# A two-layer gated cross-attention and mixture-of-experts kernel: loads in halves, grouped norms, tables asked early, and the first expert slot's columns by a permutation product

## Chip, cores and metric

One NeuronCore of a Trainium2 chip runs the whole program in one launch. The time is device microseconds (us) of an execution, the median of three runs.
## What is computed

The input x is 8 blocks of 128 tokens with 256 features; ctx_2048 has the same shape. All is float32.

```python
x = x + tanh(g_xattn[0]) * L0_xattn(layernorm(x), ctx)   # 16 heads of 16, softmax over 128 keys
x = x + tanh(g_ffn[0])   * L0_ffn(layernorm(x))          # 8 experts of 512, the best one per token
x = x + tanh(g_xattn[1]) * L1_xattn(layernorm(x), ctx)   # as L0, rms-normed queries and keys
x = x + tanh(g_ffn[1])   * L1_ffn(layernorm(x))          # causal attention 16x128, then top-6 of 16 experts
```

## The kernel before

**Stage 1, first cross-attention (0 to 89 us of the profile).** `xattn_pe`, `xattn_act`, `xattn_dve` and `xattn_pool` run with L = 0 over `steps()`, n from -3 to 8. The loop is pipelined over the blocks b: step n makes the scores of block n+1, turns the probabilities of block n (`pt`, L487), makes keys, queries and values of block n+2 (L445, L451) and turns the normalised rows of block n+3 (`normed`, L433). `first_turns` lists by hand which PSUM bank of 4 to 7 each product takes and who reads it. `keys` (ACT, L656) writes each head pair's keys masked, `queries` (L668) adds the bias; scores (L478) fill banks 0 to 3, and `softmax` (DVE, L834 and L835) reads them in two halves, subtracts the row maxima and so frees the banks for the next block's scores. `xattn_pool` makes the rows of the layer norm (`normed`, L816) from `rstd`, which `power` (L770) takes as x**-0.5 on POOL for a group of blocks at a time: for ln1 blocks 0 to 3, then 4 to 7, from `bn_stats` and `moments` that DVE makes ahead of the loop for all eight blocks. `powered` is the wait for such a group; the table POWERS gives the order.

SP issues all loads on one queue: x in two halves, the gates (16 bytes for each partition), ctx of block 0, all four weight matrices of layer 0 at once (`WX[0]`, 1 MB, semaphore wx_in[0]), `cols` (48 bytes for each partition), `vecs`, ctx of blocks 1 to 3, the router's weights, WX[1], and then the experts' weights WE. PE runs 24 products with zeros (`fill(24, 0)`, L334), then waits for WX[0] before anything else. ACT's first instruction is the tanh of the gates (L1971).

**Stage 2, first experts (89 to 216 us).** `ffn_act` and `ffn_dve` find each token's expert: exponentials (L1440), one-hot rows `hot`, the place of each token among those of its expert by products with the triangle `earlier` and with `ones` (PE, L1351 and L1353, bank 3), then `pos`, the row of each token in the list sorted by expert (L1517), and `ex`, the expert of each slot of 128 rows (L1524); there are 15 slots. `ffn_pool` waits for `pos` and scatters the 8 blocks of FX into `xs_d` in DRAM by 8 indirect DMAs (L1571); when all have landed, SP loads the rows of slots 0 and 1 (L1591), PE turns them into columns (`columns`, L1372) and the slots begin. In slot j, PE does gate product (L1378), the turn of slot j-1's hidden rows (`turn_hidden`, L1385), the columns of slot j+1 (L1372), the up product (L1378) and slot j-1's down product (L1393); gate and up take banks `par` and 2 + `par`.

While the scatter runs, PE makes keys and values of the second cross-attention for MOST = 6 blocks (`keys_values`, L1357, banks 4 to 7) from rT, for which SP loads all of ctx again once the router is done; DVE adds biases and squares (L1530, L1531, L757) and, when POOL has the power (L1574), scales the keys (`normalise_keys`, L1470). Fills of 8, 7, 10 and 2 stand around these. The last two blocks' keys and values come behind the slots.

POOL then gathers the 8 blocks from `ys_d` by indirect DMAs (L1581), with the keys' power behind block 2 and the power of ln3 for blocks 0 and 1 behind block 4. DVE's `add_experts` (L1476, L1477) adds each block to X as it lands; after blocks 6 and 7 it writes the normed rows of blocks 0 and 1 (L816), then `moments` of blocks 2 to 7, whose power POOL takes before its `normed(2)`.

**Stage 3, second cross-attention (216 to 301 us).** As stage 1 with L = 1; `fill(10, 7)` stands before it. ACT loads the activation table of the exponential on reaching the first `exps` (L676).

**Stages 4 and 5.** Causal attention (`attn_*`) and the 25 tiles of the last experts (`moe_*`), with three products for each float32r pair (L338 to L340). `moe_act` squares the columns (L1156), copies them (L1160), and loads the table of the silu on reaching the first one (L1170), for which PE's next product waits.

```python
pe.wait_ge(wx_in[0], 16)                     # stage 1, ahead of all products
sp.wait_ge(s.scattered, 16 * B)              # stage 2, SP
load(0, 0)
load(1, 1)
if b == FIRST + 2:                           # stage 2, POOL, in the loop of gathers
    power(pool, "ln3")
```

Of the kernel before, what the change touches and what calls it, by code (L numbers as in the profile page):

```python
# [23 lines left out]
P = 128  # L24
# [11 lines left out]
CTX = 4  # L36
# [3 lines left out]
J1 = SJ + E1 * I1 // P  # L40
VEC = ["bv0", "bo0", "bk1", "bv1", "bo1", "nk1"]
# [26 lines left out]
def build(nc, ctx_d, x_d, wx_d, vec_d, col_d, gate_d, rw0_d, rw1_d, moe0_d, moe1_d, attn_d, attnv_d, out_d):  # L68
    stack = ExitStack()
    with stack:  # L70
# [10 lines left out]
        WX = [sb(f"WX{i}", [P, C, 4 * D]) for i in range(2)]  # L81
# [18 lines left out]
        mhalf = sb("mhalf", [P, B])  # L100
        in_ms = sb("in_ms", [P, B])
# [46 lines left out]
        gs = [sb(f"gs{i}", [P, I0], where=e) for i in range(2)]  # L148
# [88 lines left out]
        x_in = [sem("x_in0"), sem("x_in1")]  # L237
        gate_in, vec_in, late_in, out_done = sem("gate_in"), sem("vec_in"), sem("late_in"), sem("out_done")
        wx_in = [sem("wx_in0"), sem("wx_in1")]
# [57 lines left out]
        class Es:  # L297
# [9 lines left out]
            h_ready, ht_done, ht_ready, d_done, y_ready = (sem("e_" + k) for k in ("h_ready", "ht_done", "ht_ready", "d_done", "y_ready"))  # L307
# [53 lines left out]
        def first_turns(n):  # L361

            early = [(name, 2, reader) for name, reader in (("K", "A"), ("V", "D")) if n == -1]
            late = [] if n == 0 else [("K", n + 2, "A")], [] if n == 0 else [("V", n + 2, "D")]
# [5 lines left out]
            return [*(routed(0, 1) if last else []), ("cxT", n - 1, "A"), *((f"P{i}", n, "A") for i in range(4)),  # L370
# [45 lines left out]
        def xattn_pe(pe, L):  # L416
            s, m_, W = xs[L], xbs[L], WX[L]
# [22 lines left out]
            def columns(name, b, w0, src):  # L440

                out = bank(name, b)
                for o in range(C):
                    for c in range(C):
                        m = nc.tensor.matmul(out[:, o * P:(o + 1) * P], W[:, c, w0 + o * P:w0 + (o + 1) * P], src[:, c, :], start=(c == 0), stop=(c == C - 1))  # L445
                m.then_inc(s.turn_done, 1)

            def rows(name, b, w0, src):
                out = bank(name, b)
                for c in range(C):  # L450
                    m = nc.tensor.matmul(out[:, 0:D], src[:, c, :], W[:, c, w0:w0 + D], start=(c == 0), stop=(c == C - 1))  # L451
                m.then_inc(s.turn_done, 1)

            def keys(b):
                pe.wait_ge(s.ctx_in[b % CTX], 16 * (b // CTX + 1))
                columns("K", b, 0, m_.cT[b % CTX])

            def queries(b):
                read("xT", b)
                columns("Q", b, 2 * D, m_.xT)  # L460
# [53 lines left out]
            def output(b):  # L514
                read("cxT", b)
                rows("O", b, 3 * D, m_.cxT)
# [19 lines left out]
            if L == 0:  # L536
                pe.wait_ge(Es.zeroed, 1)
                fill(24, 0)
                pe.wait_ge(psum_zeroed, 1)
                pe.wait_ge(wx_in[0], 16)  # L540
                for n in steps():
                    last, end = n == B - 1, n == B
                    if has(n + 1):
                        scores(n + 1)
                    if last:
# [18 lines left out]
                    if has(n + 2) and n != 0:  # L564
                        rows("V", n + 2, D, m_.cT[(n + 2) % CTX])
# [20 lines left out]
                    if n == -1:  # L586
                        keys(2)
                        rows("V", 2, D, m_.cT[2])
# [3 lines left out]
            fill(10, 7)  # L592
# [46 lines left out]
        def xattn_act(act, L):  # L639
# [42 lines left out]
            if L:  # L682

                for b in range(2):
                    act.wait_ge(Es.kt_free, b + 1)
# [3 lines left out]
                key_columns(act, MOST, B)  # L689
            def value_rows_back(n):  # L690
# [71 lines left out]
        POWERS = [("ln1", 0, EARLY), ("ln1", EARLY, B), ("ln2", 0, EARLY), ("ln2", EARLY, MOST), ("ln2", MOST, MOST + 1), ("ln2", MOST + 1, B), ("ln3", 0, FIRST), ("ln3", FIRST, B),  # L762
                  ("ln4", 0, B)]
        INPUTS = [(0, 2), (2, 4), (4, MOST), (MOST, MOST + 1), (MOST + 1, B)]

# [52 lines left out]
        def xattn_dve(dve, L, ch):  # L818
# [43 lines left out]
            if L == 0:  # L862
                for n in steps():
                    if has(n + 1):
                        softmax(n + 1, 0)
                    if has(n - 1) and n != B - 2:
# [3 lines left out]
                    if has(n + 2) and n != 0:  # L870
# [18 lines left out]
            for n in steps():  # L889
# [4 lines left out]
                if has(n + 1):  # L894
                    softmax(n + 1, 1)
                if B - 4 <= n < B:
# [17 lines left out]

        def xattn_pool(pool, L):
# [1183 lines left out]
```

## Time and profile before

| what | value |
|---|---|
| median of three runs | 778.97 us (778.62 to 780.02) |
| the profiled execution's own time | 778.13 us |
| its span (first to last instruction) | 776.4 us |
| mean granted TensorE clock | 0.991 of 2.4 GHz |
| PE busy | 742.0 us, 96% of the span |
| DVE, ACT, POOL busy | 54%, 44%, 32% |
| DMA | 58.04 MB, mean 75 GB/s |

Times in the profile run from the span's start. A line such as "20.38 1.15 PE PS L478 x16" is start, duration, engine, written tile, line and number of records. A float32 product leaves two records, so L478's 16 records are 8 products. The busy time of PE contains fills, products with zeros that no result needs.

### The profile page before, as it was taken

To read this page: it belongs to the slowest core of one execution; us is meant where nothing else is said; L and a number is where in the kernel's file an instruction comes from. 1 tells how busy PE (TensorE), PEld (TensorE's weight loads), DVE (VectorE), ACT (ScalarE), POOL (GpSimd) and SP (SyncE) were. 2 spreads that over 40 slices of the span, in tenths; PEclk is the share of its full clock that TensorE was granted. 3 is DMA by queue.
4 is the path that set the end of the run, shared out by engine and by line. 5 is a ranking of instruction groups with operands and counts; after the bars stand their busy time and mean duration, and the time that the engine had idled before them with its cause. 6 is when DMAs were issued, how large, how long until landed. Compare 5 with 4: busy or idle time off the path is not lost.

```text
span 776.4 us, 13496 instructions
## 1 busy us (share of the span) xinstructions
PE 742.0 (96%) x4636; PEld 605.4 (78%) x4637; DVE 421.1 (54%) x806; ACT 342.9 (44%) x813; POOL 248.7 (32%) x298
## 2 busy tenths in 40 slices
PE   8999989999869989999999999999989999999998
PEld 6787746666557767889988998898868888888886
DVE  6878451121467774544454445445564565656565
ACT  3888212222258773544454445444453332233223
POOL 5203240000444673732222321322223443444430
PEclk9999999999989999999999999999999999999999
DMA  8970221111300010101101100010014334333331
GB/s 315 420 278 2 55 81 35 47 41 41 109 15 2 1 35 1 35 22 55 35 20 34 54 20 34 20 62 21 0 41 126 97 119 115 115 114 102 115 101 55
DMA packets 25606, 58.04 MB, mean 75 GB/s; under 512 B 3536, under 2 KB 14416, under 8 KB 24288
## 3 DMA queue, kind: packets, MB, share of 16 engines
q1 hardware_dynamic: 24800, 55.42, 21.9%
q0 software_dynamic: 768, 2.10, 0.8%
q8 instruction: 25, 0.41, 0.2%
q14 instruction: 13, 0.11, 0.0%
HBM read 51.41 MB, written 6.09 MB: 74 GB/s over the span
## 4 chain that ended last, share of the span: by engine, by line
PE 80%; DVE 7%; ACT 6%; POOL 3%; DMA 2%; issue 2%; SPq 0%; DVEq 0%; POOLq 0%; ACTq 0%
PE PS L338 15%; PE PS L340 15%; PE PS L339 15%; PE PS L1636 7%; PE PS L1378 7%; PE PS L1393 3%; PE PS L445 3%; PE PS L478 2%; PE PS L487 2%; PE PS L451 2%; PE PS L1642 2%; PE PS L500 1%; POOL Z L816 1%; DVE x_mx L834 1%; PE PS L433 1%
## 5 line engine op out<-in xcount | busy, mean ns | idle before, releaser
L338 PE MATMUL PS<-tTh,wh 128*128 128x512 f32 x200 | 78.4, 392 | 1.4 <-ACT act_s L1170 0.9
L1181 ACT ACTIVATE hhh<-hh 128x512 fp32r<-128x512 f32 x50 | 31.6, 632 | 105.1 <-DVE hh L1207 94.7
L340 PE MATMUL PS<-tTh,wl 128*128 128x512 f32 x200 | 77.9, 390 | 0.0
L339 PE MATMUL PS<-tTl,wh 128*128 128x512 f32 x200 | 77.9, 389 | 0.0
L637 DVE TENSOR_TENSOR hhl<-hh,hhh 128x512 fp32r<-128x512 f32 x50 | 52.4, 1048 | 34.9 <-ACT hhh L1181 34.9
L1747 ACT ACTIVATE sm<-sm,nmx 128x128 f32<-128x128 f32 x128 | 49.6, 389 | 37.7 <-DVE nmx L1810 37.7
L1273 POOL CAST wh<-wraw 128x512 fp32r<-128x512 f32 (+1 forms) x50 | 26.1, 523 | 110.6 <-PE PS L340 110.6
L637 DVE TENSOR_TENSOR oTl<-PS,oTh 128x512 fp32r<-128x512 f32 x32 | 22.1, 691 | 71.6 <-ACT oTh L1741 71.6
L1275 POOL TENSOR_TENSOR wl<-wraw,wh 128x512 fp32r<-128x512 f32 (+1 forms) x50 | 58.0, 1160 | 8.4 <-POOL wh L1273 7.9
L1850 POOL CAST ah<-araw 128x512 fp32r<-128x512 f32 (+1 forms) x32 | 16.2, 506 | 134.4 <-PE PS L340 134.4
L1378 PE MATMUL PS<-WE,xsT 128*128 x120 | 56.4, 594 | 0.1
L338 PE MATMUL PS<-tTh,ah 128*128 128x512 f32 x128 | 53.1, 415 | 1.7 <-DVE tTl L804 1.5
L1203 DVE TENSOR_TENSOR act_s<-act_s,PS 128x512 f32<-128x512 f32 x44 | 30.2, 687 | 38.4 <-PE PS L340 38.4
L340 PE MATMUL PS<-tTh,al 128*128 128x512 f32 x128 | 50.2, 392 | 0.0
L339 PE MATMUL PS<-tTl,ah 128*128 128x512 f32 x128 | 49.9, 390 | 0.0
L834 DVE TENSOR_REDUCE x_mx<-PS 128x8 f32<-128x1024 f32 x32 | 39.0, 1217 | 12.7 <-PE PS L478 12.7
L338 PEld LDWEIGHTS PS<-tTh,wh 128*128 128x128 f32 x200 | 37.6, 188 | 10.5 <-issue 1.8
L1170 ACT ACTIVATE act_s<-PS 128x512 f32<-128x512 f32 x50 | 30.0, 599 | 32.1 <-PE PS L340 32.1
L340 PEld LDWEIGHTS PS<-tTh,wl 128*128 128x128 f32 x200 | 37.6, 188 | 7.9
L339 PEld LDWEIGHTS PS<-tTl,wh 128*128 128x128 f32 x200 | 37.6, 188 | 7.6
L1555 DVE TENSOR_TENSOR hs<-gs,PS 128x512 f32<-128x512 f32 x15 | 10.3, 687 | 54.7 <-PE PS L1378 54.7
L835 DVE TENSOR_TENSOR x_prob<-PS,x_mx 128x1024 f32<-128x1024 f32 x32 | 39.2, 1224 | 1.1
(255 smaller groups left out, 1844.0 us busy)
## 6 DMA issues: line engine op xcount, KB each, us to landing
WE<-moe SPq DMA_DIRECT2D x8, 1536.0 KB, 14.3
wraw<-moe SPq DMA_DIRECT2D x25, 384.0 KB, 3.0
araw<-attn SPq DMA_DIRECT2D x16, 384.0 KB
cwb<-cw_d SPq DMA_DIRECT2D x20, 256.0 KB, 3.9
WX<-wx SPq DMA_DIRECT2D x2, 1024.0 KB, 8.3
avraw<-attn_v SPq DMA_DIRECT2D x8, 256.0 KB
xs_d<-zeros SPq DMA_DIRECT2D x1, 1920.0 KB, 17.7
xs_s<-xs_d SPq DMA_DIRECT2D x15, 128.0 KB, 2.0
```

The source lines that it names most:

```text
L338: nc.tensor.matmul(out, wh_, xh_, start=first, stop=False, **kw)
L339: nc.tensor.matmul(out, wh_, xl_, start=False, stop=False, **kw)
L340: return nc.tensor.matmul(out, wl_, xh_, start=False, stop=last, **kw)
L637: return nc.vector.tensor_tensor(lo, src, hi.bitcast(F32), ALU.subtract)
L834: ch.link(nc.vector.tensor_reduce(m8, sc, AX.X, ALU.max))
L835: nc.vector.tensor_tensor(m_.prob[b % 2][:, 8 * g:8 * g + 8, :], sc, m8.unsqueeze(2).broadcast_to([P, 8, S]), ALU.subtract).then_inc(s.sub ...
L1181: nc.scalar.activation(hhh[half][:, :], hh[half][:, :], ACT.Copy).then_inc(s.hi_done, 1)
L1203: v.tensor_tensor(act_s[half][:, :], act_s[half][:, :], PS[:, 1, :], ALU.mult).then_inc(s.a_done, 1)
L1275: nc.gpsimd.tensor_tensor(wl[par][:, a0:a1], wraw[par][:, a0:a1], wh[par][:, a0:a1].bitcast(F32), ALU.subtract).then_inc(s.w_split, 1)
L1378: m = nc.tensor.matmul(PS[:, 2 * mat + par, :], xsT[par][:, c, :], w[:, c, :], start=(c == 0), stop=(c == C - 1))
L1636: m = nc.tensor.matmul(PS[:, si % 4, t * S:(t + 1) * S], lhs[:, a0:a0 + S], rhs[:, a0:a0 + S], start=True, stop=True)
L1747: nc.scalar.activation(sm[:, b, :], sm[:, b, :], ACT.Exp, bias=nmx[:, b:b + 1], scale=AD ** -0.5, accum_out=sums[:, b:b + 1]).then_inc(aex ...
```

## The change

Nothing is computed otherwise; the results go to the same places. In words:

1. **Loads.** x comes in three parts (blocks 0-1, 2-3, 4-7) and each layer's weights in two halves: for layer 0 Wk and Wq, then Wv and Wo. SP's order is now x 0-1, cols, ctx 0, weights half 0, gates, x 2-3, weights half 1, vecs, ctx 1 to 3, x 4-7, then as before. PE waits for half 0 at its first keys, for half 1 at the values of block 0, which move behind the scores of block 0 (and DVE's addition between the two halves of softmax 0). The first fill is 10 instead of 24.
2. **Grouped norms of layer 0.** Statistics and power are made for blocks 0-1, for 2-3, and for each of 4 to 7 alone inside steps 0 to 3 (`row_stats_of` on DVE, `power` on POOL). DVE, not POOL, makes the normed rows of blocks 0 and 1. 46 one-time memsets of routing constants move from DVE's start to POOL at n = 2.
3. **The first slot's columns by a permutation product.** From `posf` DVE makes eight 0/1 matrices `perm` (one instruction over 1024 elements), and PE multiplies FX by them into bank 5: the columns of slot 0 without the trip through DRAM. SP loads slots 1 and 2 only. Slot 0 is finished alone (gate, up, turn, down) before slot 1 begins.
4. **Keys and values** go in the order KEYS = 4, 5, 6, 7, 0 to 3: the first four blocks' ctx still lies in stage 1's buffers, so four of them need no load and fill PE's gaps around routing and permutation; two go into slot 0. The banks are 1, 7, 3 in turn. The fills of 8, 7, 10 and 2 become one of 2.
5. **Start of layer 1.** The power of ln3 is taken for blocks 0-1 behind gather 3, for 2-3 behind gather 5 and for 4-7 in the loop; the normed rows of blocks 0 and 1 follow `add_experts(3)`; `add_experts(7)` moves behind the softmax of block 0. The fill of 10 becomes 4.
6. **Tables.** Activations of one column (Exp behind the last key copies of stage 2, Silu behind the squares of stage 5) make the table loads happen there.

The core of the diff:

```diff
+KEYS = [*range(B - CTX, B), *range(B - CTX)]
@@ first_turns, xattn_pe
+            first = [("V", 0, "D")] if n == -1 else []
-            late = [] if n == 0 else [("K", n + 2, "A")], [] if n == 0 else [("V", n + 2, "D")]
+            late = [] if n == 0 else [("K", n + 2, "A")], [] if n in (-2, 0) else [("V", n + 2, "D")]
...
             def keys(b):
                 pe.wait_ge(s.ctx_in[b % CTX], 16 * (b // CTX + 1))
+                if b == 0:
+                    pe.wait_ge(wx_in[0][0], 16)
...
-                fill(24, 0)
+                fill(10, 0)
                 pe.wait_ge(psum_zeroed, 1)
-                pe.wait_ge(wx_in[0], 16)
                 for n in steps():
...
                     if has(n + 1):
                         scores(n + 1)
+                    if n == -1:
+                        pe.wait_ge(wx_in[0][1], 16)
+                        rows("V", 0, m_.cT[0])
...
-            fill(10, 7)
+            fill(4, 7)
@@ xattn_act
                 key_columns(act, MOST, B)
+
+                nc.scalar.activation(warm[:, 0:1], mhalf[:, 0:1], ACT.Exp)
@@ xattn_dve, layer 0, in the loop over n
+                    if n == -1:
+                        values(0)
...
+                    if n + EARLY in range(EARLY, B):
+                        rest_of_rows(n + EARLY)
@@ xattn_pool
             if L == 0:
                 power(pool, "ln1")
-                normed(0)
-                normed(1)
-                power(pool, "ln1", EARLY)
+                power(pool, "ln1", FIRST)
+                pool.wait_ge(s.ln_done, FIRST)
             else:
-                power(pool, "ln3", FIRST)
                 pool.wait_ge(s.ln_done, FIRST)
...
             for n in range(B):
+                if not L and n + 3 in range(EARLY, B):
+                    power(pool, "ln1", n + 3)
+                if not L and n == 2:
+                    routing_constants()
+                if L and n == 1:
+                    power(pool, "ln3", EARLY)
@@ xattn_sp
+            rows(0)
+            sp.dma_start(cols[:, :, :].rearrange("p a c -> p (a c)"), col_d).then_inc(col_in, 16)
             load(0)
-            sp.dma_start(WX[0][:, :, :], wx_d[0]).then_inc(wx_in[0], 16)
+            weights(0, 0)
+            sp.dma_start(gates[:, :], gate_d.partition_broadcast(P)).then_inc(gate_in, 16)
+            rows(1)
+            weights(0, 1)
@@ moe_act
+            nc.scalar.activation(warm[:, 1:2], mhalf[:, 1:2], ACT.Silu)
@@ ffn_pe
-            fill(8, 0)
+            nc.tensor.matmul(PS[:, 6, 0:P], ones[:, :], earlier[:, :], start=True, stop=True).then_inc(s.ids_done, 1)
+            pe.wait_ge(wx_in[1][0], 16)
+            pe.wait_ge(wx_in[1][1], 16)
+            keys_values(0)
+            fill(2, 0)
             pe.wait_ge(s.hot_done, 1)
...
+            keys_values(1)
+            pe.wait_ge(s.place_read, 1)
+            keys_values(2)
+
+            pe.wait_ge(s.perm_done, 1)
+            for c in range(C):
+                for b in range(B):
+                    m = nc.tensor.matmul(PS[:, 5, c * P:(c + 1) * P], FX[:, b, c * P:(c + 1) * P], perm[:, b, :], start=(b == 0), stop=(b == B - 1))
+            m.then_inc(s.xt_done, 1)
+            keys_values(3)
...
                 up(e, par, 0, s.g_done)
-                if not is_first(j):
+                if is_first(j):
+
+                    up(e, par, 1, s.u_done)
+                    pe.wait_ge(s.ctx_in, 16 * C)
+                    keys_values(4)
+                    turn_hidden(0)
+                    keys_values(5)
+                    down(0, 0)
+                    pe.wait_ge(s.kv_free, 2 * MOST)
+                    columns(1, 1)
+                    return
@@ ffn_dve
             v.tensor_copy(pos[:, :], posf[:, :]).then_inc(s.pos_done, 1)
+            dve.wait_ge(s.ids_done, 1)
+            v.tensor_tensor(perm, PS[:, 6, 0:P].unsqueeze(1).broadcast_to([P, B, P]), posf[:, :].unsqueeze(2).broadcast_to([P, B, P]), ALU.is_equal).then_inc(s.perm_done, 1)
@@ ffn_pool, in the loop of gathers
-                if b == FIRST + 2:
+                if b == FIRST + 1:
                     power(pool, "ln3")
+                if b == FIRST + 3:
+                    power(pool, "ln3", FIRST)
@@ vector block
-            for b in range(B):
+            for b in range(B - 1):
                 add_experts(dve, ch, b)
...
+                if b == EARLY - 1:
+                    moments(ch, FIRST, EARLY)
                     powered(dve, "ln3")
-                    ln_scale(xb1.xn[b - B + FIRST][:, :], X[:, b - B + FIRST, :], b - B + FIRST).then_inc(xs[1].ln_done, 1)
-            moments(ch, FIRST, B)
-            xattn_dve(dve, 1, ch)
+                    for k in range(FIRST):
+                        ln_scale(xb1.xn[k][:, :], X[:, k, :], k).then_inc(xs[1].ln_done, 1)
+
+            def last_rows():
+                add_experts(dve, ch, B - 1)
+                moments(ch, EARLY, B)
+
+            xattn_dve(dve, 1, ch, last_rows)
```

## Rows read from the trace of the kernel before

**Rows 1.** The page: busy time of the engines, and the chain by engine
```profile
PE 742.0 (96%) x4636; PEld 605.4 (78%) x4637; DVE 421.1 (54%) x806; ACT 342.9 (44%) x813; POOL 248.7 (32%) x298
PE 80%; DVE 7%; ACT 6%; POOL 3%; DMA 2%; issue 2%; SPq 0%; DVEq 0%; POOLq 0%; ACTq 0%
```

**Rows 2.** The chain in order of time (start, us, what), first scores of stage 1
```profile
2.88 7.81 DMA WX<-wx
...
14.19 1.16 PE PS L478 x16
...
20.38 1.15 PE PS L478 x16
```

**Rows 3.** Stretches: PE, PEld, DVE, ACT, POOL busy (x), PEclk, DMA share, GB/s
```profile
6.00:6.75 0.75, 0.75 (x5) 0.59 (x5) 0.75 (x4) 0.00 (x0) 0.00 (x0) 1.00 0.20 46
...
7.50:8.25 0.75, 0.75 (x5) 0.63 (x4) 0.72 (x6) 0.20 (x1) 0.13 (x1) 1.00 1.02 425
```

**Rows 4.** Timeline of the start: start, us, engine, line, operation, [idle before]
```profile
7.83 0.20 ACT L1971 ACTIVATE tg<-gates 128x4 f32<-128x4 f32 x1 [5.73 <-DMA gates<-gate]
8.12 1.02 POOL L770 TENSOR_TENSOR rstd<-ms,mhalf 128x4 f32<-128x4 f32 x1 [5.75 <-DVE ms L813]
...
13.87 0.42 DVE L827 TENSOR_TENSOR x_v<-PS,vecs 128x256 f32<-128x256 f32 x1 [1.45 <-PE PS L451]
...
16.62 1.22 DVE L835 TENSOR_TENSOR x_prob<-PS,x_mx 128x1024 f32<-128x1024 f32 x1
```

**Rows 5.** Timeline: VectorE in an even step of stage 1
```profile
53.99 1.22 DVE L834 TENSOR_REDUCE x_mx<-PS 128x8 f32<-128x1024 f32 x1 [0.58 <-PE PS L478]
```

**Rows 6.** Timeline: the statistics of one block alone, on VectorE
```profile
86.32 0.43 DVE L851 BATCH_NORM_STATS2 st<-X 128x6 f32<-128x256 f32 x1
...
87.00 0.15 DVE L813 TENSOR_SCALAR ms<-mv 128x1 f32<-128x1 f32 x1
```

**Rows 7.** The chain, from routing to the third expert slot
```profile
93.21 0.71 PE PS L1353 x2
...
95.82 0.23 DVE posf L1516
...
109.06 1.89 DMA xs_s<-xs_d
...
121.74 1.72 PE PS L1378 x4
```

**Rows 8.** Stretches of the routing
```profile
91.50:92.00 0.50, 0.50 (x2) 0.35 (x2) 0.43 (x3) 0.00 (x0) 0.00 (x0) 0.50 0.22 55
...
94.50:95.00 0.50, 0.50 (x4) 0.41 (x3) 0.43 (x3) 0.00 (x0) 0.00 (x0) 1.00 1.15 276
```

**Rows 9.** Timeline: keys and values of six blocks on TensorE
```profile
95.89 10.57 PE L1357 MATMUL PS<-WX,rT 128*128 128x512 f32 x24
```

**Rows 10.** The chain, from the gathers to the first softmax of stage 3
```profile
209.64 0.90 POOL rstd L770
...
212.05 2.68 DMA FX<-ys_d,pos
...
216.14 0.45 PE PS L433 x2
...
222.67 1.24 DVE x_mx L834
```

**Rows 11.** Stretches ahead of stage 3 and in its start
```profile
214.00:216.00 2.00, 0.00 (x0) 0.00 (x0) 1.67 (x5) 0.00 (x0) 0.26 (x1) 1.00 0.32 98
...
218.00:220.00 2.00, 1.56 (x8) 1.16 (x6) 0.09 (x1) 0.83 (x3) 1.61 (x2) 0.50 0.02 4
```

**Rows 12.** Timeline: two activation table loads, and the product that waits
```profile
226.42 1.28 ACT L676 ACT_TABLE_LOAD   x1
...
563.87 1.28 ACT L1170 ACT_TABLE_LOAD   x1
...
565.91 0.47 PE L338 MATMUL PS<-tTh,wh 128*128 128x512 f32 x1 [0.55 <-ACT act_s L1170]
```

More of the change, by code:

```diff
@@ L80, in build @@
         X = sb("X", [P, B, D])
-        WX = [sb(f"WX{i}", [P, C, 4 * D]) for i in range(2)]
+        WX = [sb(f"WX{i}", [P, 2, C, 2 * D]) for i in range(2)]
         head_rows = sb("head_rows", [P, HT])
@@ L147, in build @@
         xsT = [sb(f"xsT{i}", [P, C, P], where=e) for i in range(2)]
-        gs = [sb(f"gs{i}", [P, I0], where=e) for i in range(2)]
+        gs2 = sb("gs", [P, 2, I0], where=e)
+        gs = [gs2[:, i, :] for i in range(2)]
+        perm = gs2[:, :, :].rearrange("p a n -> p (a n)").rearrange("p (b s) -> p b s", b=B)
         hs = sb("hs", [P, I0], where=e)
@@ L234, in build @@
         cw_d = nc.dram_tensor("cw_d", (E1, T), F32).ap()
[L237 removed]
+        x_in = [sem(f"x_in{i}") for i in range(3)]
         gate_in, vec_in, late_in, out_done = sem("gate_in"), sem("vec_in"), sem("late_in"), sem("out_done")
[L239 removed]
+        wx_in = [[sem(f"wx_in{i}{half}") for half in "ab"] for i in range(2)]
         const_done, pairs_done, tg_done, col_in = sem("const_done"), sem("pairs_done"), sem("tg_done"), sem("col_in")
@@ L369, in first_turns @@
             last, end = n == B - 1, n == B
-            return [*(routed(0, 1) if last else []), ("cxT", n - 1, "A"), *((f"P{i}", n, "A") for i in range(4)),
+            return [*first, *(routed(0, 1) if last else []), ("cxT", n - 1, "A"), *((f"P{i}", n, "A") for i in range(4)),
                     *(routed(4) if end else []), ("O", n - 1, "D"), *late[0], ("oT", n, "A"), ("Q", n + 2, "A"), *late[1],
@@ L416, in xattn_pe, with weights @@
         def xattn_pe(pe, L):
-            s, m_, W = xs[L], xbs[L], WX[L]
+            s, m_ = xs[L], xbs[L]
+            half_of = {"K": (0, 0), "VQ"[1 - L]: (0, D), "VQ"[L]: (1, 0), "O": (1, D)}
+            def weights(name, c, a0, a1):
+                half, w0 = half_of[name]
+                return WX[L][:, half, c, w0 + a0:w0 + a1]
             def read(name, b):
@@ L563, in xattn_pe @@
                         queries(n + 2)
-                    if has(n + 2) and n != 0:
-                        rows("V", n + 2, D, m_.cT[(n + 2) % CTX])
+                    if has(n + 2) and n not in (-2, 0):
+                        rows("V", n + 2, m_.cT[(n + 2) % CTX])
                     if last:
@@ L761, in build, with group @@
         EARLY, MOST, FIRST = B // 2, B - 2, 2
-        POWERS = [("ln1", 0, EARLY), ("ln1", EARLY, B), ("ln2", 0, EARLY), ("ln2", EARLY, MOST), ("ln2", MOST, MOST + 1), ("ln2", MOST + 1, B), ("ln3", 0, FIRST), ("ln3", FIRST, B),
+        X_PARTS = [(0, FIRST), (FIRST, EARLY), (EARLY, B)]
+        POWERS = [("ln1", 0, FIRST), ("ln1", FIRST, EARLY), *(("ln1", b, b + 1) for b in range(EARLY, B)), ("ln2", 0, EARLY), ("ln2", EARLY, MOST), ("ln2", MOST, MOST + 1), ("ln2", MOST + 1, B), ("ln3", 0, FIRST), ("ln3", FIRST, EARLY), ("ln3", EARLY, B),
                   ("ln4", 0, B)]
         INPUTS = [(0, 2), (2, 4), (4, MOST), (MOST, MOST + 1), (MOST + 1, B)]
+        def group(norm, b):
+            return [(n, b0) for n, b0, b1 in POWERS if n == norm and b0 <= b < b1][0]
         def power(pool, norm, b0=0):
@@ L869, in xattn_dve @@
                         softmax(n + 1, 1)
-                    if has(n + 2) and n != 0:
+                    if has(n + 2) and n not in (-2, 0):
                         values(n + 2)
@@ L998, in xattn_sp @@
             sp.dma_start(vecs[:, 2:, :].rearrange("p a d -> p (a d)"), vec_d[2 * D:].partition_broadcast(P)).then_inc(late_in, 16)
-            sp.dma_start(WX[1][:, :, :], wx_d[1]).then_inc(wx_in[1], 16)
+            for half in range(2):
+                weights(1, half)
             for b in range(CTX, B):
@@ L1409, in ffn_pe @@
             pe.wait_ge(s.w_in, 16 * E0)
-            pe.wait_ge(s.kv_free, 2 * MOST)
-            fill(10, 0)
-            columns(0, 1)
-            fill(2, 0)
             slots(pe, tile)
@@ L1597, in tile @@
             def tile(j, par, i):
-                if not (isinstance(j, int) and j + 2 >= SLOTS):
+                if not is_first(j) and not (isinstance(j, int) and j + 2 >= SLOTS):
                     sp.wait_ge(s.xt_done, j + 1)
@@ L1925, in _ @@
         def _(sp):
-            for half in range(2):
-                b0 = half * B // 2
-                sp.dma_start(X[:, b0:b0 + B // 2, :], x_d[b0:b0 + B // 2].rearrange("b s d -> s b d")).then_inc(x_in[half], 16)
-            sp.dma_start(gates[:, :], gate_d.partition_broadcast(P)).then_inc(gate_in, 16)
             xattn_sp(sp)
@@ L2059, in cross @@
     def cross(k, v, q, o):
-        return columns(np.concatenate([m.T for m in (k, v, q, o)], axis=1))
+        return np.stack([columns(np.concatenate([m.T for m in two], axis=1)) for two in ((k, v), (q, o))])
     def expert_tiles(gate, up, down, J):
```

205 lines of the change are left out of this document (115 added, 90 removed).

## The prediction

> **What bounds the kernel now.** The page comes first: PE is busy for 96% of the span and the chain that ended last runs for 80% on PE [rows 1]. A change can gain only where PE waits or runs fills, so I went through the chain in order of time and looked for pieces that aren't PE. There are four such places, and the change touches each. In the start, the chain is the load of WX[0], which lands at 10.69, and the first scores start at 14.19 [rows 2]. In the routing, the chain goes from DVE to the scatter, and slot 0's rows arrive at 110.95; the third slot starts at 121.74 [rows 7]. Ahead of stage 3 it is gathers and additions; block 0's normed rows reach PE only at 216.14 and the first softmax starts at 222.67 [rows 10]. At the first silu of stage 5, PE waits 0.55 behind a table load [rows 12]. Everything between these places is PE's own work, so a shift at each place should pass through to the end. Small durations without a group are those of the same timelines.
>
> **Start of stage 1 (gain 3.3).** Ahead of the first weights' end stand today x (1 MB), gates, ctx 0 and 1 MB of weights. After the change it is 0.25 MB of x, cols, ctx 0 and 0.5 MB. That is 1.28 MB less, at the 425 GB/s of an undisturbed stretch [rows 3] 3.0 us: landing at 7.7 instead of 10.69. The stretch with the gates (16 bytes for each partition) moved only 46 GB/s [rows 3]; the gates now come behind the weights, so 7.7 may be up to 1.3 too late. The Trainium skill (DMA: Bandwidth & Descriptors, Specifications) says that transfers below 512 bytes are read, modified and written; this speaks against putting cols, 48 bytes for each partition, ahead of the weights. The trace agrees for the gates.
>
> The norm's chain is no longer than that: x 0-1 lands near 3.8, two statistics with their aggregation and constant take DVE about 1.2, the power 1.02 [rows 4], two normed rows on DVE 0.8, in all 6.9. What ends last is ACT: its first instruction is the tanh of the gates, at 7.83 today [rows 4], and I expect it at the same place, since less x but half the weights stand ahead. From 8.0 it is the copy of the columns (0.4), four masked keys (1.5), the query copy (0.5) and handovers: scores at 10.5, 3.7 earlier. The bounds: 9.8 if the gates land at 7.0, 12.0 if cols and gates both make slow stretches.
>
> Given back: block 0's values are now added between the two halves of softmax 0, 0.42 of DVE [rows 4]. Scores 1 wait for that softmax: from scores 0 to scores 1 are 6.2 us [rows 2], nearly all four DVE passes of 1.22 [rows 4]. So 3.7 - 0.4 = 3.3. PE's value product and the second weights (landing near 10) are hidden in the same 6.2.
>
> The statistics of blocks 4 to 7 stand in steps 0 to 3: from 86.32 to 87.15 is 0.83 for one block [rows 6]. DVE is idle for 0.58 there [rows 5]; the rest, 0.25, is taken from the next idle time of 0.5 ahead of the output, so I cost it at nothing, and if that cover is gone it is 0.25 in four steps, 1.0. On POOL the power is 1.02, and the 46 memsets at 0.05 to 0.1 are 2.3 to 4.6, ahead of the normed rows of block 5. By the step's times these rows would be ready at 41.5 to 44, and PE takes them at 43.9: nothing, or 0.1.
>
> **Routing and slot 0 (gain 4.4).** The new order on PE, from the router's end at 89.9: the index product 0.2, keys and values of one block. Six blocks are 24 records in 10.57 [rows 9], so 1.76 each. The granted clock is 0.50 (1.2 GHz) at 91.5 and again 1.00 at 94.5, after router products of 8 columns [rows 8]; in that stretch the block costs about twice as much. So the block and two fills end near 93.8, behind the one-hot rows (92.4), and the two place products, 93.21 today, end near 94.6: 0.7 later, and POOL's scatter, queued behind `pos`, is 0.7 later too. With the clock full it would be nothing.
>
> Then `pos` at 97.0; `perm` is 1024 elements from PSUM with both operands broadcast, as L835, 1.22 [rows 4], to 98.3. The product is 16 matmuls of 128 columns; a 512-column one with its two records is 0.88 [rows 9], so 0.22 each, 3.5, to 101.8. Blocks 1 and 2 of the keys fit ahead, block 3 behind (to 103.6). Slot 0: gate and up 3.5, block 4 1.76, turn 0.44, block 5 1.76, down 1.76, to 112.8; columns 1 and their copy 0.8. Slot 1 starts at 113.6. Its rows land at 110.95 + 0.7 = 111.7 [rows 7], so the scatter is hidden, by 1.1. Slot 2 follows after gate, columns and up, 3.7: 117.3 against 121.74 [rows 7], 4.4 earlier. With the full clock it is 5.2; with each of the new handovers a few tenths longer, 3.3. DVE scales six blocks' keys between slot 0 and slot 1's hidden product (six times 0.41 from 113.5): it ends at 116, before the up product at 117. Slots 2 to 14 are unchanged.
>
> **Start of stage 3 (gain 3.8).** Block 3 is added at 210.7 to 211.65. Moments of blocks 2 and 3 take 0.5, the first normed row 0.4, so PE turns it at 212.6 instead of 216.14 [rows 10]: 3.5. But the power of ln3, behind gather 3, has to wait for DVE's moments as before (209.64 today, [rows 10]), so gathers 4 to 7 are later by about 1.7, and the second power adds 0.9. Block 6 lands near 216.5, and DVE is free of it at 217.5: a floor for softmax 0, 5.2 below today's 222.67. From 216.14 to 222.67 PE ran mostly at the low clock: the row at 218 shows 0.50, after a stretch with no product at all at 214 [rows 11]. The same run from 212.6 gives 219.1 at the low clock, and the floor 217.5 at the full one. I take 218.9, gain 3.8, nearer the low clock because the fill ahead is now 4 and not 10. Block 7's addition and moments, 1.6, lie where DVE waits 1.25 for scores 1; ACT has the later end there, so I cost the rest at nothing. The table of the exponential ends at 227.70 [rows 12], hidden under the softmax that ends at 227.6 and lets the next scores go: nothing.
>
> The Trainium skill (TensorE: Matmul & The Clock Gate, Part 1) states that the slow clock is the default and that activity releases it; this speaks against cutting fills. The rows agree for the stretch at 218. By that rule alone stage 3 would gain 3.5 and the first products of stage 1 would run slow.
>
> **The silu's table (gain 0.5).** PE waits 0.55 for the first silu, which starts behind a load of 1.28 [rows 12]. The load moves to ACT's idle time behind the squares. Of the 1.28 only the 0.55 is PE's.
>
> **Sum.** 3.3 + 4.4 + 3.8 + 0.5 = 12.0. The profiled execution took 778.13, span 776.4 with 1.73 around it, and the median is 0.84 above it. From the median: 778.97 - 12.0 = 767.0.
>
> **Rivals.**
> - *All clocks full (0.2).* If the low clock in the routing and at stage 3 goes, place products are not late (5.2) and stage 3 sits on its floor (5.2): 3.3 + 5.2 + 5.2 + 0.5 = 14.2, 764.8. For it: in the routing PE's work is denser. Against it: the router's narrow products stay as they are.
> - *Clock and gathers take most of it back (0.2).* The fill of 10 ends near 6, PE then waits, and its clock is low through the start; its work of some 8 us between 7 and 20 doubles, of which the DVE passes hide half; cold products at stage 3 last into its second step. Start 1.0, routing 3.5, stage 3 2.0, silu 0.5: 7.0, 772.0.
> - *The slow side (0.02).* DVE becomes the bound of stage 1. Its place is each even step: PE's step is 8.55, DVE works about 7 of it, and the new 0.83 fits. It would decide if DVE passed 8.55, that is if a POOL instruction beside it (POOL now has the powers and 46 memsets in the loop) held DVE's passes up by over 0.7 a step. Past that point it has to pass 12.0 / 8 = 1.5 a step to eat the gain; with 3 a step, as if every pass of 1.22 took 2, it is 8 x 3 - 12 = 12 slower, 791.0. Nothing in the rows shows such a hold.
> - *The change doesn't do what it says (0.03).* If `perm` or the new waits tie slot 0 to the scatter after all, the routing gains nothing, 7.6 in all: 771.4.
> - *My forecast* has 0.55.
>
> **How the numbers follow.** The range takes in the first two rivals with their edges: 763.5 to 772.0. A measurement of this kernel tells about 0.2%, 1.6 us, from no change. All cases but the slow side and a small rest lie below 777.4: faster 0.96, same 0.02, slower 0.02.
>
> **What would show it.** First scores near 10.5 and scores 1 near 17; `perm` at 97, slot 1's gate near 113.6 in times of before less 3.3; block 0's turn 3.5 earlier against gather 0; no table load between L1160 and the first silu; the load's wait gone. It is wrong if the even step of stage 1 is longer than 8.55, if PE waits for slot 1's rows, or if the low clock lasts past stage 3's second scores.

## The result and the profile after

Four runs of the changed kernel took 764.83, 766.89, 770.28 and 770.43 us, median 768.59, beside 779.19 for the kernel before: ratio 0.986 (0.982 to 0.989). Five more, run later, have the median 767.21 (ratio 0.984, 0.981 to 0.987), which is also the median of all nine. The forecast was 767.0. In these nine runs the time falls as TensorE's mean granted clock rises: 770.28 to 771.16 at 0.984, 766.61 to 767.25 at 0.989 to 0.991, 765.95 at 0.993, 764.83 at 0.995. The trace shown first is of the run of 770.28: span 768.4, 8.0 below the span before. So its parts must show why 4.0 of the forecast 12.0 are missing there, and why another run of the same program is 5 us shorter.

The page, busy time and the chain by engine, against [rows 1]: PE's share of the chain rose from 80% to 83%, DVE, POOL, DMA and issue each lost one point.

```profile
PE 739.2 (96%) x4623; PEld 604.2 (79%) x4624; DVE 422.9 (55%) x775; ACT 343.3 (45%) x815; POOL 249.8 (33%) x347
...
PE 83%; ACT 6%; DVE 6%; POOL 2%; DMA 1%; issue 1%; SPq 0%; DVEq 0%; POOLq 0%; ACTq 0%
```

The chain in order of time (start, us, what), start of stage 1, against [rows 2]. The load of the gates has taken the place of WX[0] in it; scores 0 and 1 (L492) came at 10.21 and, in the timeline, at 17.09 instead of 14.19 and 20.38.

```profile
2.76 4.99 DMA gates<-gate
...
7.89 0.37 ACT x_xT L663
8.25 1.39 ACT x_k2T L672 x4
9.65 0.53 ACT x_qT L684 x2
...
10.21 1.15 PE PS L492 x16
```

The chain in the routing, against [rows 7]. The wait for the scatter and the load of slot 0 is gone; L1438 is the permutation product. But the keys and values of block 0 (L1418) took 3.41 and not 1.76, since the clock had already fallen at 85.3, among the router's products (before: at 90.7), and the two fills behind them (L339) took 0.85 of the chain. So the place products (L1428, L1430) were late.

```profile
87.63 3.41 PE PS L1418 x4
91.05 0.85 PE PS L339 x2
91.90 0.33 PE PS L1428 x2
92.23 0.26 PE PS L1430 x2
92.49 3.48 PE PS L1418 x8
...
96.01 3.84 PE PS L1438 x32
...
110.86 0.39 ACT xsT L1524
...
111.38 1.98 PE PS L1451 x4
```

The chain in the start of stage 3, against [rows 10]: the fill of 4 ahead of block 0's turn (L339) took 2.05, the turn is at 206.98, and queries 0 (L457) and scores 0 and 1 (L492) each took about 2.1, twice their time at full clock.

```profile
204.93 2.05 PE PS L339 x4
206.98 0.44 PE PS L445 x2
...
207.88 2.09 PE PS L457 x8
...
211.37 2.10 PE PS L492 x16
...
213.49 1.24 DVE x_mx L856
...
218.57 2.09 PE PS L492 x16
```

Stretches of the same trace (busy time of PE, PEld, DVE, ACT and POOL, then the granted clock, the DMA share and GB/s), against [rows 11]: the clock is at its lower level (1.2 GHz) throughout 206 to 214, is full again at 216, and falls a second time between 218 and 219.

```profile
206.00:214.00 8.00, 6.54 (x34) 4.64 (x33) 3.67 (x9) 2.27 (x8) 4.17 (x5) 0.50 0.19 55
...
216.00:218.00 2.00, 0.71 (x4) 0.52 (x4) 1.97 (x3) 2.00 (x6) 0.57 (x1) 1.00 0.00 0
218.00:220.00 2.00, 1.43 (x13) 1.30 (x16) 1.85 (x9) 1.59 (x2) 0.00 (x0) 0.61 0.00 0
220.00:222.00 2.00, 2.00 (x15) 1.41 (x8) 1.28 (x2) 0.00 (x0) 1.97 (x3) 0.53 0.00 0
```

The first silu of stage 5, from ScalarE's timeline, against [rows 12]: no table load ahead of it, and PE's next product, at 558.05, does not wait for it.

```profile
555.96 0.64 ACT L1221 ACTIVATE tTh<-tT 128x512 fp32r<-128x512 f32 x1
556.50 0.58 ACT L1231 ACTIVATE act_s<-PS 128x512 f32<-128x512 f32 x1
```

**The table to read everything by.** Three marks cut every trace into four parts: scores 1 of stage 1, gather 0, scores 2 of stage 3, each by its start in TensorE's or GpSimd's timeline. *Start* is up to the first mark, *routing* (most of stage 1, routing and the expert slots) to the second, *stage 3* its beginning alone, to the third, and *rest* to the end of the span. In brackets is how long the clock was low in a part (at 80 to 116, at 200 to 225, and at 275 to 292), from the granted clock of stretches of 1 us; two numbers are two stretches. Each trace is that of one run, and not always a typical one: both_warm's is its fastest (763.96, its median is 766.42), and the kernel before was traced once, while its other runs have mean clocks from 0.982 to 0.996. So gains against "before" are gains against that one trace.

| trace | start | routing (low) | stage 3 (low) | rest (low) | span |
|---|---|---|---|---|---|
| before | 20.38 | 182.46 (3.4) | 32.89 (6.8) | 540.67 (3.4) | 776.4 |
| the changed kernel | 17.09 | 179.32 (6.8) | 31.68 (10.2 and 3.4) | 540.31 (3.4) | 768.4 |
| the same, again | 16.98 | 177.18 (0) | 29.57 (3.4 and 3.4) | 540.37 (3.4) | 764.1 |
| stage3_warm | 19.17 | 177.25 (0) | 29.08 (3.4) | 540.00 (3.4) | 765.5 |
| route_warm | 16.76 | 178.19 (3.4) | 27.39 (0) | 540.16 (3.4) | 762.5 |
| both_warm | 16.87 | 177.36 (0) | 27.79 (0) | 540.08 (3.4) | 762.1 |
| no_perm | 18.17 | 189.70 (3.4 and 13.7) | 28.97 (3.4) | 540.16 (3.4) | 777.0 |
| old_stage3 | 18.55 | 177.27 (0) | 32.88 (3.4 and 3.4) | 540.50 (3.4) | 769.2 |
| no_tables | 18.13 | 178.07 (3.4) | 29.07 (6.8) | 541.93 (6.8) | 767.2 |
| gates_first | 17.49 | 179.29 (6.8) | 27.68 (0) | 540.44 (3.4) | 764.9 |
| cold | 17.93 | 178.76 (6.8) | 29.47 (13.7) | 540.34 (3.4) | 766.5 |
| last_warm | 16.89 | 178.00 (3.4) | 29.32 (6.8) | 538.99 (0) | 763.2 |
| best | 17.18 | 179.71 (6.8) | 27.65 (0) | 539.06 (0) | 763.6 |
| lean | 17.51 | 178.00 (3.4) | 27.37 (0) | 539.12 (0) | 762.0 |

### The profile page after: what moved, and what is told of

Same layout as the page of the kernel before. It is cut to its first block, busy times and chain, and to the rows that moved or that the text cites. A ratio compares the mean times of both kernels' runs of the same rounds, so it can differ in the third digit from the quotient of the medians.

```text
span 768.4 us, 13498 instructions
## 1 busy us (share of the span) xinstructions
PE 739.2 (96%) x4623; PEld 604.2 (79%) x4624; DVE 422.9 (55%) x775; ACT 343.3 (45%) x815; POOL 249.8 (33%) x347
## 4 chain that ended last, share of the span: by engine, by line
PE 83%; ACT 6%; DVE 6%; POOL 2%; DMA 1%; issue 1%; SPq 0%; DVEq 0%; POOLq 0%; ACTq 0%
PE PS L343 16%; PE PS L345 15%; PE PS L344 15%; PE PS L1730 7%; PE PS L1451 7%; PE PS L1466 3%; PE PS L457 3%; PE PS L492 2%; PE PS L501 2%; PE PS L463 2%; PE PS L1736 2%; PE PS L1418 2%; PE PS L514 1%; POOL Z L838 1%; ACT x_probT L663 1%
## 5 line engine op out<-in xcount | busy, mean ns | idle before, releaser
L1835 ACT ACTIVATE pT<-PS 128x512 f32<-128x512 f32 x32 | 17.6, 596 | 49.7 <-PE PS L1736 49.5
```

## The experiments

**First group: the clock.** Each text of what was expected sets two theories, T and R, against each other. Here T says that the missing microseconds are TensorE's low clock, R that they are the new waits. First the kernel itself once more.

> The changed kernel itself, for its spread beside the others of this call. T (what is missing of the forecast is TensorE's low clock in the routing and at the start of stage 3, which also makes runs of the changed kernel differ) expects 765 to 770.5 with the time falling by some 5 us as the mean granted clock rises from 0.984 to 0.995. R (the new waits and the gathers cost it, whatever the clock) expects the same median, but a spread of under 1 us at one clock, and low stretches of the clock at the same places in each run.

Measured: 765.95 to 771.16, median 767.21; the slowest run has clock 0.984, the others 0.989 to 0.993. Its trace has no low stretch in the routing (1.00 where the first had 0.58) and two short ones in stage 3, at other places than before. So R, which has the stretches at the same places in each run, is wrong there. Routing took 177.18, so the gain there was 182.46 - 177.18 = 5.3. The rows are the kernel of the first trace and the same kernel again:

```profile
84.00:92.00 8.00, 7.43 (x25) 4.87 (x26) 3.88 (x20) 0.79 (x3) 0.51 (x1) 0.58 0.23 68
204.00:214.00 10.00, 7.92 (x38) 5.62 (x37) 5.54 (x15) 4.12 (x10) 5.87 (x6) 0.54 0.19 52
```

```profile
84.00:92.00 8.00, 7.05 (x31) 4.26 (x32) 5.32 (x27) 0.68 (x3) 0.40 (x1) 1.00 0.23 68
204.00:214.00 10.00, 6.68 (x45) 5.18 (x44) 7.62 (x12) 4.53 (x12) 4.25 (x5) 0.83 0.13 39
```

Then fills (products with zeros) to hold the clock up:

```diff
-                    fill(15, 2)      # stage3_warm: before the last two key turns
+                    fill(20, 2)
+            fill(2, 5)               # behind the key turns
-            fill(4, 7)
+            fill(6, 7)               # also 5 before scores 0, 1 before queries 0, 3 before block 1's read of Q
+                    if end:          # route_warm
+                        fill(2, 0)   # and 2 behind routed_turn(7)
```

> More fills around the start of stage 3 alone: 5 more ahead of the last two key turns, 5 behind them, 2 more ahead of the first step, 5 ahead of scores 0, one ahead of queries 0 and 3 ahead of the read of Q in block 1. T: the stretches 206 to 214 and 218 to 222 rise from about 0.5 to near 1.0, queries 0 take 1.1 instead of 2.07, scores 0 and 1 1.1 instead of 2.09, and the kernel gains 2.0 to 3.5 on the changed one in the same call. R: the products wait for the normed rows and for handovers that don't move, so the clock rises and the time stays within 0.5, or grows by up to 1 where a fill of 0.24 stands in the path.

> Two fills ahead of the columns of the values of block 7 in stage 1's end step, and two behind each routed turn of block 7, some 1 us of fills at full clock, into time where PE waits. T: the clock no longer falls near 85, the keys and values of block 0 take 1.8 instead of 3.6, the place products come about 1 earlier, and the kernel gains 0.8 to 1.5. R: slot 0 waits for DVE's perm and POOL's scatter, so nothing moves or the fills cost up to 0.5.

> Both sets of fills. T: the gains add to 3 to 5, a median near 764.5, a mean granted clock of 0.99 or more in the profile, and a spread of the runs under 2 us instead of 5. R: within 1 us of the changed kernel, either side.

Measured: 765.77 (764.43 to 767.94), 765.33 (764.37 to 766.64) and 766.42 (763.96 to 767.57). Each median is 0.8 to 1.9 below the kernel's own run beside them, less than the spread of either, and they don't add. The trace of route_warm has the full clock in stage 3 although no fill was added there, and a low stretch of 3.4 in the routing although fills were added there. That of stage3_warm has the full clock up to 216 and a low stretch on scores 1. So the price of a low stretch shows well, but not that fills keep it away. In route_warm the part takes 27.39, and its chain shows what bounds it then: gather 6, the addition and statistics of block 6 on VectorE, and the softmax behind them, the floor of the prediction.

```profile
205.62 2.79 DMA FX<-ys_d,pos
...
208.43 0.50 DVE X L1563
...
208.95 0.43 DVE st L1564
209.37 1.13 DVE x_mx L859
...
214.35 1.15 PE PS L492 x16
```

**Second group: the parts of the change, one undone at a time.**

```diff
-            pe.wait_ge(s.perm_done, 1)
-            for c in range(C):
-                for b in range(B):
-                    m = nc.tensor.matmul(PS[:, 5, c * P:(c + 1) * P], FX[:, b, c * P:(c + 1) * P], perm[:, b, :], start=(b == 0), stop=(b == B - 1))
...
+            columns(0, 1)
             pe.wait_ge(s.experts_done, 1)
```

> Slot 0's columns come from DRAM again, after the scatter and a load, everything else is as in the changed kernel (the order of the keys and values too). From gather 0 less scores 1 of stage 1: 182.46 before, 179.3 with the changed kernel's low clock and 177.2 without it. T (the product is what saves the wait for scatter and load, 5.2 against the kernel before at full clock): slot 0's rows come some 2 after the scatter has landed at 107.7, its gate starts near 110.6 instead of 101.4, and nothing else can stand in, so this stretch takes 186.4 to 188.5, 9.2 more than the changed kernel at the same clock, and the median is 775 to 778. R (the keys and values in their new order hide most of the wait, and the product itself brings little): the stretch stays under 182.5 and the median under 771.

Measured: 780.92 (779.01 to 785.48, 10 runs), as slow as the kernel before (ratio 1.0024, 1.0005 to 1.0042) and slower than both theories said. The chain goes through the eight scatters:

```profile
104.80 2.40 DMA xs_d<-FX,pos
107.22 2.05 DMA xs_s<-xs_d
...
110.56 5.91 PE PS L1446 x8
```

Slot 0's gate starts 92.4 behind scores 1 instead of 84.3: 8.1 of wait, near T's 9.2. Then gate and up took 5.91 instead of 3.43, since PE had stood for 10.76 and the clock had gone low: 2.5 more, which T had not counted. The part takes 7.2 more than before: the kernel before had six blocks of keys and values ahead of slot 0 and the new order has four, so without the product the new order costs about what the halves and groups gained.

```diff
-                if b == FIRST + 1:              # old_stage3, POOL in the loop of gathers
+                if b == FIRST + 2:
                     power(pool, "ln3")
-                if b == FIRST + 3:
-                    power(pool, "ln3", FIRST)
...
-            moments(ch, EARLY, B)               # DVE: the last addition ahead of the loop again, then
+            moments(ch, FIRST, B)               # one group of moments for blocks 2 to 7
...
-            fill(4, 7)
+            fill(10, 7)
```

> Ahead of stage 3 the additions, moments, powers and fills stand as in the kernel before (one power for all blocks behind the last addition); halved loads, product and the new product order of the step stay. From scores 2 of stage 3 less gather 0: 32.89 before, 31.7 in the changed kernel with two spells of low clock, 29.1 to 29.6 with one, 27.4 to 27.8 with none. T: the stretch is 31.5 to 33 in the profile, whatever the clock of the changed kernel, and the median is 1 to 4 above the changed kernel's, 768.5 to 771. R (the gathers set the start in any order): within 0.5 of the changed kernel's 31.7, and the medians agree within 1.

Measured: 771.00 (770.16 to 771.64); stage 3 took 32.88 to the 32.89 of before, with as much of the low clock. T. Its first scores stand 17.1 behind gather 0 and 17.7 in the kernel before, but 12.9 to 13.5 in the nine traces of the new order whose first low stretch comes later than scores 0 (all but the first, cold and no_perm): 3.5 to 4.2 is the order's own.

```diff
-                nc.scalar.activation(warm[:, 0:1], mhalf[:, 0:1], ACT.Exp)    # no_tables
-            nc.scalar.activation(warm[:, 1:2], mhalf[:, 1:2], ACT.Silu)
```

> The two small activations that ask for a table early are left out. T: PE's wait of 0.5 to 0.6 at the first silu of stage 5 is back, and the load of Exp ahead of the first softmax of stage 3 lies beside DVE's reduce and subtraction (2.4 long against 1.28), so nothing is lost there: the end less scores 2 of stage 3 grows from 540.2 to 540.7, and the median by 0.5, within the spread. R: both loads stand in the chain, 1.28 each, and the kernel is 1.8 to 2.5 slower.

Measured: 768.38 (765.18 to 768.99). PE's wait at the first silu is back (0.54). From the router's product in stage 5 to the end are 212.1 here and before, 211.4 with the change: 0.7 for the silu's table. The other 0.9 by which the 541.93 is above the changed kernel's 540.3 goes with a low stretch at 275 of 6.8 where it is 3.4 elsewhere. The median is 1.2 above 767.21, within the spread. The load of Exp is hidden, as T had it: it starts beside VectorE's softmax, and scores 1 come no later than elsewhere (6.3 behind scores 0).

```profile
213.53 1.28 ACT L692 ACT_TABLE_LOAD   x1
```

```diff
             rows(0)
+            sp.dma_start(gates[:, :], gate_d.partition_broadcast(P)).then_inc(gate_in, 16)     # gates_first
...
             weights(0, 0)
-            sp.dma_start(gates[:, :], gate_d.partition_broadcast(P)).then_inc(gate_in, 16)
```

> The load of the four gates for all partitions (16 bytes a partition) goes right behind the first blocks of X, ahead of cols, context and weights of the cross-attention. T (ACT waits for the gates' load until 7.8 in the changed kernel, and PE's products for the weights until 6.9): ACT is free near 6.5, but the weights come some 0.5 later, so PE stands longer and its products run at the low clock more often; scores 0 at 9.7 to 11, scores 1 within 0.7 of 17.0, the median within 0.7. R (the slow small rows delay whatever stands behind them by their whole 1.3): the weights land at 7.9 or later, scores 1 at 18 or later, and the kernel is 1 to 2 slower.

Measured: 765.50 (764.55 to 766.75), 1.7 below the 767.21 of the changed kernel, which was not run beside it, and the ranges overlap. The gates land at 4.2, PE's first product with the weights starts at 6.99, so R is wrong; scores 0 come at 10.16. Scores 1 come at 17.49, since the next late load is in the chain now, the bias vectors' that VectorE waits for:

```profile
4.22 7.63 DMA vecs<-vec
...
11.88 0.35 DVE vecs L2115
...
17.49 1.15 PE PS L492 x16
```

**Third group: the other direction, and one more low stretch.**

```diff
-            fill(2, 0)        # cold: behind keys_values(0)
-                    fill(15, 2)
-            fill(4, 7)
```

> The other direction: the fills of the changed kernel between the routing and the first step of stage 3 are left out (2 behind the keys and values of block 0, 15 ahead of the last two key turns, 4 ahead of the first step), nothing else. T (where PE waits, its clock goes low, and the products behind run at half speed): from gather 0 less scores 1 of stage 1 at 179.3 or above, scores 2 less gather 0 at 31.5 to 35, at least 9 of the whole microseconds from 80 to 100 and 200 to 225 under 0.98 of the clock, and the median 1.5 to 5 above the changed kernel's 767.2. R (the clock spells are by chance and don't follow from what PE does there): median within 1 of 767.2.

Measured: 767.47 (765.82 to 768.59), no slower than with the fills. T falls on its median. The clock did stay low, from 202 to 216, the longest stretch of any trace there:

```profile
204.00:214.00 10.00, 7.07 (x36) 5.10 (x36) 6.02 (x16) 4.24 (x10) 5.89 (x6) 0.50 0.18 52
```

Yet the part took 29.47. Against a full clock, the way to scores 0 cost 1.2 more in it and from there to scores 1 0.9; from scores 1 to scores 2 are 8.0, as with a full clock. In the changed kernel's first trace these are 1.9, 0.9 and 1.5. The 1.5 is the second low stretch, which cold did not have. The 0.7 between 1.9 and 1.2 is the fill of 4 itself: at the low clock it took 2.05 and held up block 0's turn, which came 0.68 behind its normed rows, while in cold PE waited for these rows:

```profile
206.34 0.66 PE L445 MATMUL PS<-ident,x_xn 128*128 128x128 f32 x2 [1.46 <-DVE x_xn L837]
```

In the routing, too, cold (178.76) is 0.5 below the other traces of its order with 6.8 of low clock (179.32, 179.29), whose chain passes through the two fills. So cold does not tell that a low clock costs nothing. Its edit did two things: what PE lost by the clock, it got back by the fills that no longer stood in the path. What a low stretch costs hangs on the products and fills that it falls on, not on its length alone.

```diff
+                if n == B - 1:         # last_warm: the step of block 7 in stage 3
+                    fill(8, 0)
```

> 8 fills ahead of the values' columns in the step of block 7 of stage 3 alone, where PE waits 2.4 for DVE's last division and every trace so far, the one of before too, has a low clock for 3.5 to 7.5 right behind (275 to 292). T: that spell is gone, the end less scores 2 of stage 3 falls from 540.2 to 538.2 to 538.8, and the median by 1.5 from 767.2. R (what follows there waits for ACT and DVE): the spell goes, and the end less scores 2 stays at 540 or above.

Measured: 765.66 (763.28 to 767.29); rest 538.99 against 540.0 to 540.5, 1.0 to 1.5 of gain, a little less than T had. The low stretch at 275 to 292 is gone in this trace and in both later ones with the edit, and is there in all 11 traces without it:

```profile
273.34 2.09 PE L339 MATMUL PS<-zeros 128*128 128x512 f32 x8
276.00 0.44 PE L445 MATMUL PS<-ident,x_cx 128*128 128x128 f32 x2 [0.57 <-DVE x_cx L864]
276.28 1.91 PE L501 MATMUL PS<-ident,x_prob 128*128 128x128 f32 x16
```

L501's 16 records took 1.91 there, and 2.63 in both_warm.

best is both_warm, gates_first and last_warm together.

> All that helped, together: both sets of fills, the 8 in the last step of stage 3, and the gates' load ahead. T: scores 1 at 17 to 17.7, 177.3 to gather 0, 27.5 to scores 2, 538.5 to the end: a span of 761, a median of 763 to 764.5, below each of the parts, and the mean granted clock at 0.996 or above. R (fills only trade one wait for another, as the 766.4 of both sets together says): a median of 765.5 to 766.5.

Measured: 765.05 (764.65 to 767.01), between T's range and R's. Stage 3 is as T had it (27.65) and the rest nearly (539.06, T 538.5), but the routing had 6.8 of low clock in spite of its fills and took 179.71, the longest of the traces with the product.

lean is gates_first and last_warm alone.

> The changed kernel with only two of the edits: the gates' load ahead, and the 8 fills in the last step of stage 3. None of the fills around the routing and the start of stage 3. T, as the runs so far have left it (those fills settle nothing: the spells there come and go with them and without them, and each costs 0.5 for every microsecond at half clock in the routing and 1.6 to 2.2 in stage 3): scores 1 at 17.2 to 17.5, to gather 0 177.3 (no spell) to 179.3 (the long one), to scores 2 27.5 to 29.6, to the end 539.0, and the median within 1 of the 765.05 of all edits together. R (those fills do carry a part): the median is 1.5 or more above that, 766.5 or higher.

Measured: 764.41 (761.97 to 768.76, 6 runs; ratio to before 0.9813, 0.9789 to 0.9838). T: the added fills of the first group carry nothing that can be told. (The expectation's 0.5 for every microsecond of low clock in the routing is twice too much: most traces of the routing show 0.2 to 0.3.) This is the fastest version of the study by its median, though its interval overlaps those of the others; its fastest run, 761.97, has the clock at 1.000 throughout, its slowest, 768.76, at 0.987.

## Why the prediction came out as it did

**Start of stage 1: right.** Forecast scores 0 at 10.5 and a gain of 3.3 at scores 1; measured 10.21 and 3.29, with ACT ending last behind the gates' tanh (7.77), as said. That the 3.3 came out so exactly is luck: scores 0 were 4.0 earlier and not 3.7, and 0.7 was given back and not 0.4, because DVE's first softmax stood behind an instruction that waits for the load `vecs`, a wait that the forecast did not have:

```profile
11.27 0.56 DVE L2115 TENSOR_SCALAR vecs<-vecs,tg 128x256 f32<-128x256 f32 x1 [1.13 <-DMA vecs<-vec]
```

And the load is not the same in every run: in 5 of the 10 traces of this load order PE's first product with WX's first half starts by 6.9, in the others at 7.9 to 8.5, and in those scores 1 come at 17.9 to 19.2, a gain of 1.2 to 2.5. Scores 0 of stage3_warm, at 12.41, are beyond the forecast's bound of 12.0. Why the load is late in some runs stays open. With the gates ahead it was there by 7.0 in three of three. The Trainium skill (DMA: Bandwidth & Descriptors, Specifications) gives 512 bytes as the least transfer for the full rate; these traces tell that small rows cost little ahead of the large loads.

**Statistics and memsets in the steps: right.** Cost nothing: the even step is still 8.55 (scores at 23.85 and 32.40).

**Routing: mechanism right, one term mis-sized.** "The two place products ... 0.7 later" took the clock's fall at 90.7 from the trace before; here it fell at 85 and covered more products, and they ended 1.9 late. The gain was 3.1 in that trace and not 4.4, which is 1.3 of the missing 4.0. With the clock full (again, stage3_warm, both_warm, old_stage3) the routing takes 177.2 to 177.4, a gain of 5.1 to 5.3 where 5.2 was forecast; with 3.4 low it is 178.0 to 178.2, with 6.8 178.8 to 179.7. Slot 1's rows were waited for in no trace that has the product, so the scatter is hidden, and no_perm shows that the product hides it.

**Stage 3: right in its two ends, low for this trace.** Block 0's turn came 2.9 earlier against gather 0 (by the timeline 206.78 - 196.41 = 10.37, before 13.30), forecast 3.5. In the ten other traces with the product and with this order of stage 3 it came 3.2 to 3.9 earlier. The floor of 5.2 was right: with a full clock the part takes 27.4 to 27.8, 5.1 to 5.5 less than before. The step that failed is "the same run from 212.6 gives 219.1 at the low clock": it gave the low clock one stretch, as in [rows 11]; there were two, and the second, on scores 1, cost 1.5 that no term had. The fill of 4 at the low clock, ahead of block 0's turn, cost another 0.7 and was in no term either: the forecast took it only as a reason for a fuller or a lower clock. One of the forecast's own signs of being wrong, a low clock past the second scores, was there: these ended at 220.7, the stretch at 221.9. The gain was 1.2 in that trace, and 3.3 and 3.8 in the next two traces. The sentence on the Trainium skill's rule (TensorE: Matmul & The Clock Gate, Part 1) against cutting fills is not borne out beyond the spread: cold's four runs have mean clocks of 0.984 to 0.989, the changed kernel's nine 0.984 to 0.995, and the time was not longer. No trace has a low clock in the start of stage 1, with its fill cut from 24 to 10.

**Silu: right.** 0.5 forecast, 0.7 measured.

**The sum.** 3.3 + 3.1 + 1.2 + 0.4 = 8.0 in the first trace. (The 0.4 is the silu's 0.7 less 0.3 somewhere between scores 2 and stage 5, which I have not traced.) The rival with all clocks full, 764.8, is what the best runs give (764.83); the forecast lies between the two kinds of run, and so in the middle of their spread; that the median of all nine is within 0.2 of it is in part luck. The rival that took most back by the clock had its place wrong: nothing ran slow in the start, but two stretches fell in the routing and stage 3. No trace shows stage 1 bound by VectorE.

What stays open: what decides whether a low stretch comes in the routing and at scores 1. The same program has it in one run and not in the next, and none of the sets of fills tried there settles it. No run undoes the halved loads or the grouped norms of stage 1 alone, so their gain is read from the traces and not from an experiment.

## What to carry to other kernels

Cut the traces at the same marks and compare parts: a change that looks 4 us short of its forecast here was right in each part in the main, less the low stretches of TensorE's clock and the fills that they stretched, and one trace alone would have had me explain chance. Price such stretches at both levels before a change whose work stands behind a wait, and fill a wait that is there in every run (2.4 us before block 7's last columns) rather than those that come and go: a fill ends in time at the full clock and can stand in the path at the low one. Filling a wait with other work (keys and values here) is no substitute for removing it: with the new order kept and the product alone taken out, the whole gain was gone.

## What the runs showed of the hardware that was not expected

- Each of the 14 traces has a stretch at the low clock, of 3.4 to 13.7 us, and two runs of one program have them at different places. In the changed kernel's first trace one began at 85.3, among the router's products of 8 columns, after PE had been busy for 3.29 of the 3.30 us from 82.0 at the full clock. So a busy PE does not exclude it:

```profile
82.00:85.30 3.30, 3.29 (x29) 3.01 (x27) 1.66 (x5) 0.77 (x2) 0.56 (x1) 1.00 0.00 0
```

- A microsecond of low clock cost 0.2 to 0.35 us in the routing (0.8 for 3.4, 1.5 to 2.0 for 6.8, 2.4 in best), and in stage 3 from 0.15 (cold, 2.1 for 13.7, with the fills gone from the path) to 0.5 (stage3_warm, 1.7 for 3.4), by what it fell on.
- The load of 16 bytes for each partition took 2.7 to 2.9 us from issue to landing right behind the first blocks, and 4.6 to 5.9 behind the weights.
- Runs of one program spread by up to 6.8 us (lean), more than its start (2.9) or its routing (4.5) gained; the mean clock of the longest run is 0.987, that of the shortest 1.000.
